# Rewriting the five engine orders of a software-pipelined decoder layer, with three scratch rows for the squared deviations

## What is computed

```python
x = _layernorm(x + _L0_attn_ref(x, Wqkv, q_norm_w, k_norm_w, Wo), axis=-1)   # 16 heads of 32, RMS-norm and RoPE on q and k, causal
x = _layernorm(x + _L0_xattn_ref(x, ctx_2048, ctx_2048), axis=-1)            # 8 heads; features against features, over 16 "depth" rows
x = _layernorm(x + _L0_ffn_ref(x, L0_ffn_weight), axis=-1)                   # fp8-style quantise/dequantise per 128 elements, then x @ W.T
```

## Time and profile before

| what | value |
|---|---|
| median of three runs | 2799.9 us |
| profiled execution | 2798.56 us, of which span 2796.8 us |
| PE busy | 2586.9 us (92%) |
| DVE busy | 2252.9 us (81%) |
| ACT busy | 2030.6 us (73%) |
| POOL busy | 1535.7 us (55%) |
| mean granted TensorE clock over the span | 0.964 |

### The profile page before, as it was taken

How to read it: one execution, slowest core, us unless ns; L and a number is a source line. 1 busy time by engine, 2 the same in 40 slices (tenths; PEclk the granted TensorE clock), 3 DMA queues, 4 the chain that set the end, 5 groups by cost and what they waited for, 6 DMA issues and landing times.

```text
span 2796.8 us, 65074 instructions
## 1 busy us (share of the span) xinstructions
PE 2586.9 (92%) x19088; PEld 1156.4 (41%) x19088; DVE 2252.9 (81%) x3405; ACT 2030.6 (73%) x2945; POOL 1535.7 (55%) x2393
## 2 busy tenths in 40 slices
PE   0679999999999999999999999999999999999774
PEld 0444444444444444444444444444444444444211
DVE  6247888888888888888888888888888888888751
ACT  0235777887778778887888777877887788777653
POOL 1243556655665556655665566655665566556422
PEclk9779999999999999999999999999999999999866
DMA  2133344434443344434343444334443444344211
GB/s 88 38 82 96 93 115 100 118 96 113 109 111 100 106 118 101 110 97 120 99 117 95 114 106 114 100 105 118 102 109 96 121 99 115 98 115 98 84 37 30
DMA packets 534121, 278.46 MB, mean 100 GB/s; under 512 B 401057, under 2 KB 483105, under 8 KB 534049
## 3 DMA queue, kind: packets, MB, share of 16 engines
q1 hardware_dynamic: 534048, 277.56, 38.4%
...
...
## 4 chain that ended last, share of the span: by engine, by line
PE 79%; DVE 5%; POOL 5%; ACT 4%; issue 4%; DMA 4%; SPq 0%; ACTq 0%; DVEq 0%; POOLq 0%
PE bank L912 27%; PE pv L1042 15%; PE mx L1015 9%; PE st L1029 9%; PE bank L1051 6%; ACT pp L601 3%; PE bank L979 2%; PE bank L961 2%; DMA xdT<-xd 2%; PE bank L948 2%; PE bank L905 2%; PE bank L951 2%; PE bank L982 2%; DVE nm L761 1%; POOL yq L561 1%
## 5 line engine op out<-in xcount | busy, mean ns | idle before, releaser
L761 DVE TENSOR_REDUCE nm<-mx 128x2 f32<-128x1024 f32 x1024 | 1252.3, 1223 | 265.7 <-PE mx L1015 245.5
L601 ACT ACTIVATE pp<-st,esc 128x1024 f32<-128x1024 f32 x1024 | 1139.7, 1113 | 321.5 <-PE st L1029 259.7
L1042 PE MATMUL pv<-pp,vT 128*32 128x512 f32 x4096 | 550.4, 622 | 0.4 <-ACT pp L601 0.2
L1029 PE MATMUL st<-qp,kp 50*128 50x512 f16 x2048 | 402.8, 390 | 36.2 <-ACT pp L601 34.5
L1015 PE MATMUL mx<-kp,qp 48*128 48x512 f16 x2048 | 401.8, 389 | 28.1 <-DVE nm L761 26.6
L912 PE MATMUL bank<-w_h,xT_h 128*128 128x512 f32 x768 | 349.9, 456 | 4.8 <-DVE xT_l L807 4.7
L912 PE MATMUL bank<-w_l,xT_h 128*128 128x512 f32 x768 | 308.1, 401 | 0.0
L912 PE MATMUL bank<-w_h,xT_l 128*128 128x512 f32 x768 | 305.8, 398 | 0.0
L1015 PEld LDWEIGHTS mx<-kp,qp 48*128 48x128 f16 x2048 | 99.3, 93 | 373.6 <-DVE nm L761 189.9
L912 PEld LDWEIGHTS bank<-w_h,xT_h 128*128 128x128 f32 x768 | 146.6, 191 | 169.8 <-issue 135.7
L528 POOL TENSOR_SCALAR_AFFINE_SELECT p<-p 128x512 f32<-128x512 f32 x256 | 162.9, 636 | 95.1 <-ACT p L644 95.0
...
## 6 DMA issues: line engine op xcount, KB each, us to landing
...
xb<-x SPq DMA_DIRECT2D x64, 256.0 KB, 2.6
x_rows<-x SPq DMA_DIRECT2D x64, 256.0 KB, 2.1
q_rows<-qpl SPq DMA_DIRECT2D x64, 256.0 KB, 2.8
cx<-ctx SPq DMA_DIRECT2D x64, 256.0 KB, 2.8
k_rows<-kpl SPq DMA_DIRECT2D x64, 256.0 KB, 2.8
x<-x_rows SPq DMA_DIRECT2D x64, 256.0 KB, 2.8
```

What stands on the lines that cost most here:

```text
L601: a.activation(pp[:, unit % 2, 2 * l:2 * (l + 1), :], st[:], ACT.Exp, scale=esc[b.i][:])\
L761: v.tensor_reduce(cols, mx[:], AX.X, ALU.max, negate=True).then_inc(mx_free, 1)
L1029: last = t.matmul(st[:, q, :], kp[b.i][rows, p, i * P:(i + 1) * P], qp[b.i][rows, p, :], start=True, stop=True)
L1042: last = t.matmul(pv[32 * j:32 * j + 2 * XD, :], vT[b.i][:, i, GROUPS * j + g, :], pp[:, unit % 2, j, :], start=(i == 0), stop=(i == KC - 1))
```

## The change

No operation is added, removed or altered. `junkd` becomes three rows, one for each layer norm, and the five tables and the bank table are written anew. The tables now start at another point of the slot, so the stage numbers differ by one in many places though the step is at the same point of the pipeline; the largest stage is 7 instead of 8, which gives 71 slots with 52 in the loop. Since a line was added twice above the steps, a step's line number is 2 higher in the changed kernel than before.

```diff
-        junk, junkc, junkd = sb("junk", [P, D], BF16), sb("junkc", [P, D], BF16), sb("junkd", [P, D], BF16)
+        junk, junkc = sb("junk", [P, D], BF16), sb("junkc", [P, D], BF16)
+        junkd = [sb(f"junkd{i}", [P, D], BF16) for i in range(3)]
...
         SP_STEPS = steps("""
-            ld_cx:0@3 ld_qp:1@4 ld_kp:1@4 ld_x:0@0 turn_xd:0@7 ld_x2r:0@6 st_kpl:0@3 ld_qp:0@3
-            st_sh1:0@1 st_x2:0@2 st_out:0@7 ld_kp:0@3 ld_sh1:0@1 st_sh2:0@4 ld_sh2:0@4 turn_parts:0@0
-            turn_parts:1@0 st_qpl:0@2""")
+            ld_qp:0@4 st_sh2:0@5 st_x2:0@3 ld_sh2:0@5 turn_parts:0@1 ld_cx:0@3 turn_parts:1@1
+            ld_kp:1@4 ld_qp:1@4 st_qpl:0@3 turn_xd:0@7 ld_x:0@0 st_kpl:0@3 ld_x2r:0@6 st_sh1:0@1
+            ld_kp:0@3 st_out:0@7 ld_sh1:0@1""")
...
         BANK = {
-            "xT": 2, "q": 2, "k": 1, "v": 0, "s1m0": 1, "s1m1": 0, "s1m2": 1, "s1m3": 1, "s1t0": 2,
-            "s1t1": 2, "s1t2": 1, "s1t3": 1, "pvo": 2, "pvs": 0, "wo": 0, "vT": 1, "ffn": 0, "ct": 1}
+            "xT": 0, "q": 0, "k": 1, "v": 0, "s1m0": 0, "s1m1": 1, "s1m2": 2, "s1m3": 2, "s1t0": 2,
+            "s1t1": 2, "s1t2": 1, "s1t3": 1, "pvo": 2, "pvs": 0, "wo": 2, "vT": 1, "ffn": 1, "ct": 2}
...
-                a.activation(junkd[:], rows[:], ACT.Square, bias=neg_mean[i][:], accum_out=devs[i][:]).then_inc(s_devs[i], 1)
+                a.activation(junkd[i][:], rows[:], ACT.Square, bias=neg_mean[i][:], accum_out=devs[i][:]).then_inc(s_devs[i], 1)
```

More of the change, by code:

```diff
@@ L198, in post_ln_decoder_kernel @@
-        DVE_STEPS = steps("""
-            self_max:2@2 cross_max:11@5 add_ffn:0@8 self_max:3@2 self_shift:0@2 cross_max:12@5
-            add_cross:0@7 cross_max:13@5 rope_terms:0@1 cross_max:14@5 cross_turn:0@6 cross_max:15@5
-            ctx_inv:0@5 cross_shift:0@5 cross_max:0@4 quant_scale:0@7 rope_terms:1@1 cross_max:1@4
-            cross_max:2@4 quant_magic:0@7 cross_max:3@4 self_recip:0@2 self_norm:0@2 cross_max:4@4
-            cross_max:5@4 cross_turn:1@6 cross_max:6@4 add_self:0@2 cross_max:7@4 self_max:0@1
-            cross_max:8@4 ctx_exp:0@3 self_max:1@1 cross_max:9@4 xT_low:0@0 cross_max:10@4""")
@@ new lines, in post_ln_decoder_kernel @@
+            part_low:1@1 quant_round:0@7 oT_low:0@2 quant_round:1@7 quant_round:2@7 query_low:0@3
+            cross_scale:0@6 xd_low:0@7 layer_mean:0@2 ctx_scale:0@3 cross_scale:1@6 context_low:0@3
+            layer_mean:2@7 layer_rstd:2@7 layer_mean:1@6 layer_rstd:0@2 mean_square:0@0
+            layer_rstd:1@6 rope_sum:0@0 mean_square:1@0 part_low:0@0 quant_unit:0@6 mask:0@1 mask:1@1
+            rope_sum:1@0 mask:2@1 mask:3@1""")
+        ACT_STEPS = steps("""
+            context_high:0@3 probs:4@5 probs:5@5 xT_high:0@0 layer_devs:0@2 probs:6@5 layer_devs:2@7
+            probs:7@5 layernorm:2@7 probs:8@5 layer_devs:1@6 square:0@0 probs:9@5 layernorm:0@2
+            probs:10@5 layernorm:1@6 square:1@0 self_probs:0@1 part_high:0@0 probs:11@5
+            self_probs:1@1 query_high:0@2 value:0@0 probs:12@5 self_probs:2@1 probs:13@5
+            self_probs:3@1 part_high:1@0 probs:14@5 probs:15@5 oT_high:0@1 probs:0@4 context_out:0@3
+            probs:1@4 probs:2@4 ctx_square:0@2 xd_high:0@6 probs:3@4""")
@@ new lines, in post_ln_decoder_kernel @@
+        DVE_STEPS = steps("""
+            self_norm:0@2 cross_max:4@4 cross_turn:1@6 cross_max:5@4 cross_max:6@4 add_self:0@2
+            cross_max:7@4 ctx_exp:0@3 self_max:0@1 cross_max:8@4 self_max:1@1 self_max:2@1
+            cross_max:9@4 xT_low:0@0 cross_max:10@4 self_max:3@1 add_ffn:0@7 cross_max:11@4
+            self_shift:0@1 cross_max:12@4 add_cross:0@6 cross_max:13@4 cross_turn:0@5 cross_max:14@4
+            rope_terms:0@0 cross_max:15@4 quant_scale:0@6 cross_shift:0@4 cross_max:0@3
+            rope_terms:1@0 cross_max:1@3 cross_max:2@3 quant_magic:0@6 ctx_inv:0@4 cross_max:3@3
+            self_recip:0@1""")
@@ new lines, in post_ln_decoder_kernel @@
+        PE_STEPS = steps("""
+            proj_v:2@1 proj_v:3@1 cross_scores_T:12@6 cross_scores:1@4 cross_pv:4@6 self_pv:0@2
+            self_scores_T:2@2 self_pv:1@2 cross_scores:2@4 cross_scores_T:13@6 self_scores_T:3@2
+            cross_pv:5@6 cross_scores:3@4 cross_scores_T:14@6 self_pv:2@2 self_pv:3@2 cross_pv:6@6
+            cross_scores_T:15@6 context_T:0@4 cross_scores:4@4 cross_scores_T:0@5 cross_pv:7@6
+            cross_scores:5@4 cross_scores_T:1@5 proj_o:0@2 proj_o:1@2 cross_scores_T:2@5
+            cross_scores:6@4 proj_o:2@2 proj_o:3@2 cross_scores_T:3@5 cross_scores:7@4
+            self_scores:0@1 self_scores:1@1 ctx_sum:0@3 cross_scores_T:4@5 cross_scores:8@4
+            cross_pv:0@5 cross_pv:1@5 self_scores:2@1 cross_scores:9@4 cross_scores_T:5@5 ffn:0@7
+            x_T:0@0 ffn:1@7 cross_scores_T:6@5 cross_scores:10@4 self_scores:3@1 ffn:2@7 ffn:3@7
+            cross_scores_T:7@5 cross_scores:11@4 proj_q:0@0 proj_q:1@0 cross_scores:12@4 cross_pv:2@5
+            cross_pv:3@5 cross_scores:13@4 cross_scores_T:8@5 proj_q:2@0 proj_q:3@0
+            cross_scores_T:9@5 cross_scores:14@4 proj_k:0@0 proj_k:1@0 cross_scores_T:10@5
+            cross_scores:15@4 proj_k:2@0 proj_k:3@0 self_scores_T:0@1 proj_v:0@0 cross_scores:0@3
+            cross_scores_T:11@5 proj_v:1@0 self_scores_T:1@1""")
```

25 lines of the change are left out of this document (removed).

## The result

The kernel with the new orders takes 2805.1 us (median of 20 runs, 2801.2 to 2812.8) against 2799.7 of the kernel before in the same comparison (20 runs). The ratio is 1.0025 with a 95% interval of 1.0016 to 1.0034: slower by a quarter of a per cent, less than the 0.3% that I had set as the bound of "no change", but clearly not nothing. The forecast was 2799, and the time lies in its range.

What follows compares the result with a forecast made beforehand. PE was taken as the bound, busy 39.17 of a 39.35 us slot. Terms of -0.23, 0.0, +0.11, -0.14 and +0.25 gave -0.01 per slot, times 64 -1 us: 2799 us, range 2770 to 2828.

Steps and rivals of the forecast that it cites:

- (b4): PE's wait at x_T for the load of x, now issued behind the transpose turn_xd: +0.25 us per slot, bounds 0 and +0.7.
- DVE comes in time: DVE, 34.5 us busy in 39.4, reaches each cross_max in time except where said; no cost in the sum.
- (a): PE's own steps beside new neighbours: 0.15 gained by a second back-to-back cross_pv pair, 0.08 by others; -0.23 us per slot.
- (b1): Wait behind self_scores_T:2 goes (-0.2), a new one of 0.2 to 0.3 comes at self_pv:3; net 0.0 us per slot.
- (b2): Stretch from self_pv:3 to proj_o: chain stays 4.94, PE's work falls to 4.51; +0.11 us per slot, bounds 0 and +0.2.
- (b3): The loop's turn on SP no longer delays the load of cx: -0.14 us per slot, bounds -0.14 and 0.
- the two lengths: Slots of 39.35 and 39.63 us, the 0.28 between them laid to the loop's turn; foretold within 0.1 after the change.
- a wait on `nm`: Sign on PE that DVE has become too dense, if a slot's mean came out above the foretold bounds.
- Fill and drain: Filling and draining the pipeline: same chains, more cross_pv in a row may cost a few us; 0, bounds -6 and +8.
- the test: Forecast counted as wrong if a slot's mean lies outside 39.4 to 39.65 us.
- the row of `x_T`: Sign on PE at x's transposes: if the slot's mean is above the bounds, it tells whether the load is the cause.

Runs made afterwards that it cites:

- x_first: Changed kernel with SP's load of x issued ahead of the transpose turn_xd instead of behind it; 2791.2 us, ratio 0.9971 to the kernel before.
- ct_back: Changed kernel with context_T and cross_pv:6 exchanged on PE, back to the order of the kernel before; 2799.0 us, ratio 1.0001 to the kernel before.
- cx_early: Kernel before with SP's load of cx moved from first step behind the loop's turn to near the end of the table; 2792.2 us, ratio 0.9979.
- xT_later: Changed kernel with x_T behind ffn:1 on PE instead of between ffn:0 and ffn:1; 2806.3 us, ratio 1.0023 to the kernel before.
- drain_alt: Changed kernel with cross_pv:0 behind cross_scores_T:3 in the last four slots alone; 2796.9 us, ratio 0.9992 to the kernel before.
- x_cs8: Changed kernel with load of x and transpose ahead of st_qpl on SP, plus cross_pv:0 ahead of cross_scores:8 on PE; 2793.3 us, ratio 0.9980 to the kernel before.

## Why the forecast was wrong, step by step

The forecast was a change of -1 us; the kernel is 5 us slower, clear of the noise. Two steps of the sum failed: the wait for the load of x, (b4), was taken too small, and "DVE comes in time" was put at nothing. That the time came out near 2799 is in part luck, for the gain of the steps, the waits, the fill and the drain were each missed by 6 us or more, in both directions.

**The steps, (a): right in kind, too small.** The waits read from start to start over 26 batches add up to 0.74 before and 1.46 after, which leaves 38.80 and 38.27 for the steps: a gain of 0.5 where I had 0.23. Besides the pair `cross_pv:0`, `:1` (0.14), `cross_pv:4` followed by a `self_pv` costs 0.88 rather than 1.00, `x_T` between two parts of `ffn`, where it doesn't wait (x_first), 0.44 rather than 0.57, and `context_T` 0.59 rather than 0.67.

**(b1) right.** The wait behind `self_scores_T:2` is gone, and `self_pv:3` waits 0.19, at the edge of the 0.2 to 0.3 that I gave. Net -0.05 for my 0.0.

**(b2) right in mechanism, larger.** The chain from `self_pv:3` to `proj_o:0` was taken as 4.94 and measured 5.04 on the mean (5.01 before); with 4.43 of PE's work beside it (I had 4.51) the waits in it are 0.61, and 0.39 before: +0.22 for my +0.11. ct_back shows that it is the chain and not the place.

**(b3) right in mechanism, a little smaller.** ACT no longer waits for `cx`:

```profile
1061.35 0.62 ACT L610 ACTIVATE junkc<-cx 128x512 bf16<-128x512 f32 x1
```

cx_early puts the price at 0.11, the forecast at 0.14. I had read the whole difference of the two lengths as the loop's turn; on the mean it is 0.33 before, of which 0.19 lies at `ffn:0` and the rest in the chain to `proj_o:0`. The two lengths are now within 0.1 (39.76 and 39.68 over 15 slots of each kind), as foretold, but partly by chance: the waits at `x_T` and at `cross_scores:8` still alternate from slot to slot, by 0.09 and 0.17, one up where the other is down.

**(b4) is the term that was mis-sized.** It was 0.25 and measured 0.48. The load is issued 0.38 behind the end of the transpose's issue, not 0.31, it lands after 2.77 us, not 2.6, and `x_T` starts 0.12 behind the landing: 4.53 from the issue of the transpose, where I had 4.16. `ffn:0` stands at 3.43 and not at 3.17, so `x_T` could have started at 4.09 (I had 3.83, and 0.1 of slack): 0.44 in this slot. x_first confirms the cause: with the load ahead the wait at `x_T` is gone.

**"DVE comes in time" failed.** At `cross_scores:8` it doesn't, for `cross_max:7` is behind `add_self`: 0.17 a slot that stood in no term. I had said that a wait on `nm` would show DVE as too dense; it shows with 1.2 us of idle in 26 slots before the pairs into `mx`, unnamed. Density isn't the reason, though: `add_self` itself waits for `proj_o` (0.54 in the slot shown), so DVE is idle just before, and the new order of PE leaves 1.7 us of PE's work from `cross_scores:7` to `cross_scores:8` where it had 2.1. xT_later shows the like: of what PE gains at `x_T` alone, 0.40 is taken back by DVE's chain some 5 us later. So even with (b4) at its true size the waits don't simply add, which no list of single waits tells.

**Fill and drain.** I put 0 with bounds of -6 and +8, and said that more `cross_pv` in a row may cost a few us there. The drain cost 6 to 8, most of which drain_alt gives back; x_cs8 speaks for the place of `cross_pv:0` behind `cross_scores_T:4` as what costs, rather than the two in a row. The fill gave 7 to 10, beyond the bound of -6; a good part of that goes with the granted clock, and its cause isn't known. Of the slots' +0.19 (by 64, +12) the runs therefore show less than half.

**The range.** Its -0.45 to +0.45 is not the sum of the terms' bounds, as the forecast has it; those add up to -0.69 and +0.90.

**Together:** foretold -0.23 for the steps and +0.22 for the waits, measured -0.53 and +0.72. Of the 0.50 by which the waits were more, 0.23 are (b4), 0.17 are DVE's, 0.11 are (b2), and (b1) and (b3) nearly cancel. The slot's mean of 39.72 is outside the 39.4 to 39.65 that I had set as the test, and the row of `x_T` names the load, as I said it would in that case.
